# First attention rows behind the last down product, two query projections in the first group's slots

## The chip, the cores and the metric

One core of a Trainium2 chip. The metric is device microseconds for one execution of the whole kernel.

## The reference

x is 4 batches of 512 tokens of 512 values, ctx another such tensor. In four steps x gets:

```python
x = x + tanh(g_xattn[0]) * wkv_scan(layernorm(x), ctx)            # L0 attention
x = x + tanh(g_ffn[0])   * bitlinear_ffn(layernorm(x))            # w1, w2 (2048 wide), silu, w3
x = x + tanh(g_xattn[1]) * cross_attention(layernorm(x), ctx)     # L1, 16 heads of 32
x = x + tanh(g_ffn[1])   * ternary_linear(rmsnorm(layernorm(x)))

# cross_attention
q = qdq(x) @ qdq(wq).T + bq                   # qdq: round to int8 by the row's maximum, and back
k, v = split(cond @ wkv.T + bkv)
attn = softmax(einsum(q, k) * scale)
out = qdq(einsum(attn, v)) @ qdq(wp).T + bp
```

## The kernel before

Each engine has its program written out by hand in one function, and the engines are ordered by semaphores; every engine works strictly in its written order, so a wait holds all that is behind it on that engine.

The tokens are 16 row tiles (TOK) of 128. The first stage (to about 200 us) is the scan and the keys and values. The second is the two-layer network over the 16 tiles, tile by tile, with an `up` product in four pieces and a `down` product in four pieces. Under it, some tiles behind, run the query steps of the second attention for tile u: `q_stats` (mean and variance, VectorE), `q_rstd` (GpSimd), `q_norm` (ScalarE), `q_max` (row maximum, VectorE), `q_diag` (GpSimd), `q_round` (ScalarE), `q_ints` (VectorE), `q_turn` (TensorE transposes, and a product with ones that spreads the scale, bank 4), `q_operands` (ScalarE copies both out), `q_project` (16 matmuls of 128x128 on WQT, bank 7), `q_full` (VectorE, out of bank 7), `q_bias` (ScalarE, four pieces and a cast), `q_low` (GpSimd, the rest after rounding to 16 bits), `store_q` (SyncE, to DRAM). Tiles 13, 14 and 15 (TOK - 3 to TOK - 1) have these steps behind the network's end.

The third stage is the attention: 4 batches of 4 groups (b, g) of 4 heads, 16 groups, each with 16 slots (t, j), t a block of 128 keys and j a head. Ahead of a group, `rows` computes 16 products of queries and keys (banks 0, 1, 5 in turn) and VectorE's `maxima` takes the maximum of each (line 1682). `c_turn` (TensorE), `c_out` (ScalarE) and `c_low` (VectorE) make of them two rows c, which `send_c` (SyncE) puts beside the queries. In a slot, `scores` (line 1211) computes keys times queries with c and with the ones of `ones_under` (GpSimd) as further rows, ScalarE takes the exponential (line 957), `weigh` (line 1221) multiplies by the values, and GpSimd's `add_weights` (line 676) adds the exponentials of the four key blocks, head by head, 12 adds a group, into the buffers ACC. `sum_weights` (line 1233, slot 5 of the next group) sums them over the keys. The rows of the next group run in the slots (`coming`, 6 of them ahead). One rule ties the score of slot n to the exponential of slot n - 2, as there are two banks. The last stage (from about 830 us) is the output projection and the last linear layer.

The exponentials have eight buffers PR, the sums two sets ACC[0] and ACC[1], used by turns. Before, ACC[0] lies in low memory and ACC[1] in XQT, QF and QB, of which QF and QB are the buffers of `q_full` and `q_bias`. SyncE, once the last `up` product is done, loads keys, values and queries of the first batch's four groups, sends c of the first two groups, stores the queries of tiles 11 to 15, waits for the stores, and goes on with the loads of the next batch.

On TensorE, the order behind the last down product (tile 15) is `q_project(13)`, `q_turn(14)`, rows 0 to 2, `q_project(14)`, rows 3 and 4, `q_turn(15)`, rows 5 to 7, `q_project(15)`, rows 8 to 15, `c_turn(0, 0)`.

Of the kernel before, what the change touches and what calls it, by code (L numbers as in the profile page):

```python
# [60 lines left out]
def flamingo_kernel(nc, x, ctx_2048, g_xattn, g_ffn, w, u, w1, w2, w3, wq, bq, wkv, bkv, wp, bp, gamma, wl, out):  # L61
    stack = ExitStack()
    with stack:
# [61 lines left out]
        def part(count, dt, pat=None, **kw):  # L125
# [4 lines left out]
            if dt == F32:  # L130
# [57 lines left out]
        ACC = [[part(SEQ, F32) for _ in range(HG)],  # L188
               [a.bitcast(F32).rearrange("p n t -> p (n t)") for a in XQT] + [a.rearrange("p k t -> p (k t)") for a in (QF, QB)]]
# [152 lines left out]
        def _(sp):  # L342
# [152 lines left out]
            for u in range(TOK - DB - 1, TOK):  # L495
                store_q(u)
            sp.wait_ge(q_out, 32 * TOK)

            def feed(b, first, last):
                for g in range(DB):  # L500
                    at_b, at_g = (b, DB - 1) if g == 0 else (b + 1, g - 1)
                    if not (first and g == 0 or last and g > 0):
                        load_kv(at_b, at_g, False)
                        load_q(at_b, at_g)
                    if not (first and g == 0 or last and g == DB - 1):
                        send_c(*following(b, g))

# [12 lines left out]
        def _(pool):  # L520
# [125 lines left out]
            def ones_under(g):  # L646

                pool.wait_ge(b_ps, FC * TOK)
                pool.wait_ge(diag3, TOK)
                if g > 0:  # L650
                    pool.wait_ge(q_lo, TOK - DB + 1 + g)
                nc.gpsimd.memset(KS[96:98, HG * g:HG * g + HG, :], 1.0).then_inc(ks_ones, 1)
                pool.wait_ge(ks_ones, g + 1)
# [3 lines left out]
            q_low(TOK - 4)  # L657
            q_diag(TOK - 2)
            q_rstd(TOK - 1)
            q_diag(TOK - 1)  # L660
            ones_under(0)
            for u in (TOK - 3, TOK - 2, TOK - 1):
                q_low(u)
                ones_under(u - TOK + 4)

            def add_weights(b, first, last):
                for g in range(DB):
                    n, acc = b * DB + g, ACC[g % 2]
                    for t in range(1, TB - 1 if last and g == DB - 1 else TB):
                        for j in range(HG):  # L670
                            pool.wait_ge(exp_done, n * 16 + HG * t + j + 1)
                            if t == 1:
                                up_to(pool, sum_ps, n - 1)
                            else:
                                pool.wait_ge(acc_done, n * 12 + HG * (t - 2) + j + 1)
                            nc.gpsimd.tensor_tensor(acc[j], PR[j] if t == 1 else acc[j], PR[(HG * t + j) % 8],  # L676
                                                    ALU.add).then_inc(acc_done, 1)

# [21 lines left out]
        def _(act):  # L700
# [220 lines left out]
            q_operands(TOK - 1)  # L921
            q_bias(TOK - 2)
            q_bias(TOK - 1)
# [23 lines left out]
            def attend(b, first, last):  # L947
                for g in range(DB):
                    n = b * DB + g
                    opening, closing = first and g == 0, last and g == DB - 1  # L950
                    for t in range(TB):

                        up_to(act, pv_tile, n * TB + t - 1)
                        for j in range(HG):
                            up_to(act, acc_done, n * 12 + (j - 7, j - 3, j + 1, j + 1)[t])
                            act.wait_ge(st_ps, n * 16 + HG * t + j + 1)
                            nc.scalar.activation(PR[(HG * t + j) % 8], bank[2 + j % 2][:, :], ACT.Exp,  # L957
                                                 scale=SCALE).then_inc(exp_done, 1)
                            if (t, j) == (0, 3) and not opening:
                                ot_out(*preceding(b, g))  # L960
                            if (t, j) == (1, 3) and not opening:
                                sums_out(*preceding(b, g))
                            if (t, j) == (2, 1) and not closing:
                                c_out(*following(b, g))

# [51 lines left out]
        def _(pe):  # L1017
# [127 lines left out]
            def q_turn(u):  # L1145

                pe.wait_ge(li3, u + 1)
                up_to(pe, lt_out, u)
                for k in range(DB):
# [45 lines left out]
            def c_turn(b, g):  # L1195
                n = b * DB + g
                pe.wait_ge(row_max, n * 16 + 16)
                up_to(pe, den_ready, n - 2)
# [26 lines left out]
            def sum_weights(b, g, final=False):  # L1225

                n = b * DB + g
                pe.wait_ge(acc_done, n * 12 + (8 if final else 12))
                if not final:
# [37 lines left out]
            def attend(b, first, last):  # L1267
                for g in range(DB):
                    opening, closing = first and g == 0, last and g == DB - 1
                    ahead = coming(b, g)  # L1270
                    for slot in range(16):
# [6 lines left out]
                        if slot == 1 and not opening:  # L1278
                            weigh(*preceding(b, g), TB - 1)
                        if slot == 5 and not opening:  # L1280
# [18 lines left out]
            q_project(TOK - 3)  # L1299
            q_turn(TOK - 2)  # L1300
# [3 lines left out]
            q_project(TOK - 2)  # L1304
            first_rows(3, 5)
            q_turn(TOK - 1)
            first_rows(5, 8)
            q_project(TOK - 1)
            first_rows(8, 16)
            pe.wait_ge(down_read, TOK)  # L1310
            pe.wait_ge(h_done, FC * TOK)
            pe.wait_ge(qf_ready, TOK)
# [52 lines left out]
        def _(dve):  # L1365
# [341 lines left out]
            def attend(b, first, last):  # L1707
                for g in range(DB):
                    opening, closing = first and g == 0, last and g == DB - 1
                    ahead = coming(b, g)  # L1710
                    for slot in range(16):
# [4 lines left out]
                        if slot == 12:  # L1716
                            bias_row(b * DB + g)
                        if slot == 14 and not opening:
# [21 lines left out]
            q_full(TOK - 3)  # L1740
            link(ts(LSC, LSC, 1.0 / 127.0, None, ALU.mult))
            ts(LSC, LSC, TG[:, 3:4], None, ALU.mult).then_inc(area_free, 1)
            q_max(TOK - 1)
            first_maxima(0, 2)
            q_full(TOK - 2)
            q_ints(TOK - 1)
            first_maxima(2, 8)
            q_full(TOK - 1)
# [110 lines left out]
```

## Time and profile before

| | |
|---|---|
| median of 3 runs | 932.35 us (931.32 to 932.54) |
| the profiled execution | 932.0 us |
| its span | 930.3 us |
| mean granted clock of TensorE | 0.956 of full |
| busy TensorE, VectorE, ScalarE, GpSimd | 86%, 81%, 62%, 60% |

All times in rows are microseconds from the start of the span, of one profiled execution. In a row of a timeline the first number is the start, the second the time until the merged instructions (x4 is four) end, and in brackets stands the idle time of the engine ahead of them and what ended it. Matmul ends are modelled, and a row of one engine may overlap the next by the depth of its pipeline.

### The profile page before, as it was taken

The page shows a single profiled execution, that of the slowest core. Times are in us where ns is not written, and L with a number is a line of the kernel's source. Part 1 is how long each engine was busy: PE and PEld are TensorE (multiplying, and loading weights), DVE is VectorE, ACT ScalarE, POOL GpSimd, SP SyncE. Part 2 cuts the span into 40 slices and gives each one's busy share as a digit, 9 for nine tenths or more (in the row PEclk, how much of TensorE's full clock was granted, in tenths as well). Part 3 has the DMA queues.
Part 4 walks back from the last instruction along what each step waited for, and adds up shares of the span by engine and source line. Part 5 has one row for each costly group of instructions (what it writes and reads, how often), then busy time and mean ns, then how long its engine had stood idle before and what let it go on. Part 6 is the DMA issues. An engine that isn't in the chain of part 4 may idle for free.

```text
span 930.3 us, 14313 instructions
## 1 busy us (share of the span) xinstructions
PE 803.7 (86%) x4253; PEld 349.7 (38%) x4253; DVE 757.6 (81%) x1510; ACT 573.2 (62%) x974; POOL 553.6 (60%) x604
## 2 busy tenths in 40 slices
PE   3798997789999989999999987999999999855663
PEld 3454453334344444444444443232323232222221
DVE  4999998778899899899888768787888888634885
ACT  4878886543566565666666554666666666646762
POOL 7756753223334444444444344899999999955661
PEclk9999999799999999999999995999999999997886
DMA  9978875533353353354333455413131311000111
GB/s 306 248 203 221 220 184 162 135 88 69 61 120 58 79 114 77 72 80 80 80 69 71 77 119 109 102 47 92 47 92 47 91 47 47 2 1 0 46 68 68
DMA packets 186985, 90.70 MB, mean 97 GB/s; under 512 B 138640, under 2 KB 171552, under 8 KB 186912
## 3 DMA queue, kind: packets, MB, share of 16 engines
q1 hardware_dynamic: 186592, 89.82, 40.2%
q8 instruction: 33, 0.54, 0.3%
q14 instruction: 40, 0.33, 0.1%
q10 hardware_dynamic: 320, 0.01, 0.0%
HBM read 44.05 MB, written 16.78 MB: 65 GB/s over the span
## 4 chain that ended last, share of the span: by engine, by line
PE 34%; DVE 24%; issue 10%; ACT 7%; POOL 4%; DMA 0%; DVEq 0%; SPq 0%; ACTq 0%; POOLq 0%
PE bank L1129 11%; PE bank L1141 5%; PE bank L1221 4%; POOL B L676 4%; PE bank L1211 4%; PE bank L1192 4%; DVE bank L1556 3%; DVE gsm L1558 3%; DVE B L1567 3%; DVE B L1561 2%; DVE B L1682 2%; PE bank L1339 2%; ACT bank L830 2%; ACT A L957 2%; DVE gsm L1559 1%
## 5 line engine op out<-in xcount | busy, mean ns | idle before, releaser
L1129 PE MATMUL bank<-A,B 128*128 128x512 f16 x1024 | 233.1, 381 | 13.3 <-DVE B L1567 12.7
L607 POOL TENSOR_TENSOR B<-B 128x512 f16<-128x512 f32 x64 | 75.7, 1183 | 218.1 <-DVE B L1567 132.2
L1682 DVE TENSOR_REDUCE B<-bank 128x1 f32<-128x512 f32 x256 | 161.5, 682 | 42.5 <-PE bank L1192 42.2
L957 ACT ACTIVATE A<-bank 128x512 f32<-128x512 f32 x256 | 142.5, 602 | 81.9 <-PE bank L1211 79.8
L676 POOL TENSOR_TENSOR B<-B,A 128x512 f32<-128x512 f32 x124 | 160.6, 1330 | 0.0
L1129 PEld LDWEIGHTS bank<-A,B 128*128 128x128 f16 x1024 | 99.2, 98 | 139.3 <-DVE B L1567 15.7
L1141 PE MATMUL bank<-A,B 128*128 128x512 f16 x512 | 120.7, 379 | 0.0
L830 ACT ACTIVATE bank<-B 128x512 f32<-128x512 f32 x64 | 38.5, 602 | 130.5 <-DVE B L1561 130.5
L1211 PE MATMUL bank<-A 98*128 98x512 f16 x256 | 95.7, 386 | 9.8 <-ACT A L957 8.1
L1192 PE MATMUL bank<-A 96*128 96x512 f16 x256 | 98.6, 403 | 5.3 <-DVE B L1682 3.6
L676 POOL TENSOR_TENSOR B<-A 128x512 f32<-128x512 f32 x64 | 79.9, 1272 | 12.7 <-ACT A L957 12.3
L1221 PE MATMUL bank<-A,B 128*32 128x512 f32 x512 | 68.2, 604 | 2.4 <-ACT A L957 1.0
L1141 PEld LDWEIGHTS bank<-A,B 128*128 128x128 f16 x512 | 49.5, 98 | 54.3 <-DMA B<-B 0.4
L1104 PE MATMUL bank<-B 128*128 128x512 f16 x192 | 50.0, 416 | 20.0 <-DVE B L1448 19.9
L1556 DVE SCALAR_TENSOR_TENSOR bank<-bank,ffs,B 128x512 f32<-128x512 f32 x64 | 48.4, 755 | 12.9 <-PE bank L1129 11.6
L1567 DVE SCALAR_TENSOR_TENSOR B<-bank,gsm 128x512 f32<-128x512 f32 x64 | 44.2, 691 | 16.1 <-ACT bank L830 14.0
L825 ACT ACTIVATE B<-bank,ffs 128x512 f32<-128x512 f32 x64 | 43.2, 675 | 18.8 <-PE bank L1129 18.5
L559 POOL TENSOR_SCALAR B<-X,mv,rs 128x128 f32<-128x128 f32 x64 | 54.1, 858 | 0.4
L1192 PEld LDWEIGHTS bank<-A 96*128 96x128 f16 x256 | 25.1, 100 | 67.8 <-DVE B L1682 49.3
L593 POOL TENSOR_TENSOR B<-B 128x512 f16<-128x512 f32 x16 | 18.9, 1180 | 47.4 <-ACT B L804 40.3
L1211 PEld LDWEIGHTS bank<-A 98*128 98x128 f16 x256 | 24.9, 98 | 58.6 <-ACT A L957 38.3
L1558 DVE TENSOR_REDUCE gsm<-bank 128x8 f32<-128x512 f32 x64 | 44.3, 692 | 2.2
(215 smaller groups left out, 1463.7 us busy)
## 6 DMA issues: line engine op xcount, KB each, us to landing
B<-in_L_ffn_w_dram SPq DMA_DIRECT2D x48, 256.0 KB, 3.5
A<-k_parts SPq DMA_DIRECT2D x48, 128.0 KB, 2.6
A<-q_parts SPq DMA_DIRECT2D x48, 128.0 KB, 3.6
X<-in_x_dram SPq DMA_DIRECT2D x4, 1024.0 KB, 8.9
B<-in_ctx_dram SPq DMA_DIRECT2D x16, 256.0 KB, 5.2
k_parts<-B SPq DMA_DIRECT2D x16, 256.0 KB, 4.2
v_rows<-B SPq DMA_DIRECT2D x16, 256.0 KB, 2.7
q_parts<-B SPq DMA_DIRECT2D x32, 128.0 KB, 2.2
```

The lines of the kernel that those rows point to most:

```text
L607: nc.gpsimd.tensor_tensor(HLb[j][:, 1, :], Db[j % 2], HLb[j][:, 0, :], ALU.subtract).then_inc(lo_done, 1)
L676: nc.gpsimd.tensor_tensor(acc[j], PR[j] if t == 1 else acc[j], PR[(HG * t + j) % 8], ALU.add).then_inc(acc_done, 1)
L957: nc.scalar.activation(PR[(HG * t + j) % 8], bank[2 + j % 2][:, :], ACT.Exp, scale=SCALE).then_inc(exp_done, 1)
L1129: last = mm(bank[2 * n + q][:, :], XQT[a][:, m, :], wt[:, m % DB, j * 512:j * 512 + 512], start=(m == 0), stop=(m == 2 * DB - 1))
L1141: last = mm(bank[5 + q][:, :], HT[j][:, m, :], W3T[:, DB * j + m % DB, :], start=(j == 0 and m == 0), stop=(j == FC - 1 and m == 2 * DB - 1))
L1192: mm(bank[ROW_BANKS[r % 3]][:, :], QS[0:96, HG * g + j, t * P:t * P + P], KS[0:96, HG * g + j, :], start=True, stop=True).then_inc(row_ps, 1)
L1211: mm(bank[2 + j % 2][:, :], KS[0:98, HG * g + j, t * P:t * P + P], QS[0:98, HG * g + j, :], start=True, stop=True).then_inc(st_ps, 1)
L1221: last_ = mm(bank[6][DH * j:DH * j + DH, :], VB[:, t, (HG * g + j) * DH:(HG * g + j + 1) * DH], PR[(HG * t + j) % 8], start=(t == 0), stop ...
L1556: stt(H, H, C2, SAb[q], ALU.mult, ALU.mult).then_inc(h_done, 1)
L1558: link(reduce(gsm[:, 0, :], grouped(H), AX.X, ALU.max, apply_absolute_value=True))
L1567: stt(grouped(Db[q]), grouped(bank[q][:, :]), RND, spread(1), ALU.subtract, ALU.mult).then_inc(d_done, 1)
L1682: reduce(NMX[g % 2][:, t, j:j + 1], bank[ROW_BANKS[r % 3]][:, :], AX.X, ALU.max, negate=True).then_inc(row_max, 1)
```

## The change

TensorE now starts the first group's rows directly behind the last down product: rows 0 to 2, `q_project(13)`, rows 3 to 5, `q_turn(14)`, rows 6 to 15. `q_project(14)`, `q_turn(15)` and `q_project(15)` go to slots 2, 4 and 7 of the first group (`opening`). The steps of the other engines for these tiles follow into the slots, GpSimd's low part of tile 14 between its adds of t = 1 and t = 2 of the first group and that of tile 15 ahead of the second group's adds. As QF and QB are now in use during the first group, the buffers ACC move: ACC[1] takes WQT, which is free once `q_project(15)` is done. GpSimd's memsets of the ones come earlier, ahead of the low part of tile 13. SyncE stores tiles 14 and 15 behind the send of c for the third group.

```diff
-        ACC = [[part(SEQ, F32) for _ in range(HG)],
-               [... XQT] + [... (QF, QB)]]
+        low = [part(SEQ, F32) for _ in range(HG)]
+        wq_halves = WQT[:, :, :].rearrange("p k d -> p (k d)").bitcast(F32).rearrange("p (h s) -> p h s", h=2)
+        ACC = [low[0:2] + [a.bitcast(F32).rearrange("p n t -> p (n t)") for a in XQT],
+               low[2:4] + [wq_halves[:, h, :] for h in range(2)]]
...
@@ sync
-            for u in range(TOK - DB - 1, TOK):
+            for u in range(TOK - DB - 1, TOK - 2):
                 store_q(u)
-            sp.wait_ge(q_out, 32 * TOK)
...
                         send_c(*following(b, g))
+                    if first and g == 1:
+                        store_q(TOK - 2)
+                        store_q(TOK - 1)
+                        sp.wait_ge(q_out, 32 * TOK)
@@ gpsimd
             q_low(TOK - 4)
+            pool.wait_ge(q_lo, TOK - 3)
+            ones_under(0)
+            pool.wait_ge(ks_ones, 1)
             q_diag(TOK - 2)
             q_rstd(TOK - 1)
             q_diag(TOK - 1)
-            ones_under(0)
-            for u in (TOK - 3, TOK - 2, TOK - 1):
-                q_low(u)
-                ones_under(u - TOK + 4)
+            pool.wait_ge(diag3, TOK)
+            for g in range(1, DB):
+                ones_under(g)
+            pool.wait_ge(ks_ones, DB)
+            q_low(TOK - 3)
...
                     n, acc = b * DB + g, ACC[g % 2]
+                    if first and g == 1:
+                        q_low(TOK - 1)
+                        pool.wait_ge(qp_ps, TOK)
...
+                        if first and g == 0 and t == 1:
+                            q_low(TOK - 2)
@@ scalar
             q_bias(TOK - 3)
-            q_operands(TOK - 1)
-            q_bias(TOK - 2)
-            q_bias(TOK - 1)
...
+                            if (t, j) == (1, 1) and opening:
+                                q_operands(TOK - 1)
+                            if (t, j) == (1, 3) and opening:
+                                q_bias(TOK - 2)
+                            if (t, j) == (3, 1) and opening:
+                                q_bias(TOK - 1)
@@ tensor
+                if u == TOK - 1:
+                    pe.wait_ge(ct_ready, 1)
+                    pe.wait_ge(ct_low, 1)
...
                 pe.wait_ge(row_max, n * 16 + 16)
+                if n < 2:
+                    pe.wait_ge(lt_out, TOK - 1 + n)
...
                 pe.wait_ge(acc_done, n * 12 + (8 if final else 12))
+                if n == 0:
+                    pe.wait_ge(qf_ready, TOK)
...
+                        if slot == 2 and opening:
+                            q_project(TOK - 2)
+                        if slot == 4 and opening:
+                            q_turn(TOK - 1)
+                        if slot == 7 and opening:
+                            q_project(TOK - 1)
...
-            q_project(TOK - 3)
-            q_turn(TOK - 2)
             pe.wait_ge(d_done, FC * TOK)
             pe.wait_ge(down_read, TOK - 1)
             first_rows(0, 3)
-            q_project(TOK - 2)
-            first_rows(3, 5)
-            q_turn(TOK - 1)
-            first_rows(5, 8)
-            q_project(TOK - 1)
-            first_rows(8, 16)
+            q_project(TOK - 3)
+            first_rows(3, 6)
+            q_turn(TOK - 2)
+            first_rows(6, 16)
             pe.wait_ge(down_read, TOK)
             pe.wait_ge(h_done, FC * TOK)
-            pe.wait_ge(qf_ready, TOK)
             c_turn(0, 0)
@@ vector
+                        if slot == 3 and opening:
+                            q_ints(TOK - 1)
+                        if slot == 5 and opening:
+                            q_full(TOK - 2)
+                        if slot == 10 and opening:
+                            q_full(TOK - 1)
...
-            q_full(TOK - 3)
             link(ts(LSC, LSC, 1.0 / 127.0, None, ALU.mult))
             ts(LSC, LSC, TG[:, 3:4], None, ALU.mult).then_inc(area_free, 1)
+            first_maxima(0, 3)
             q_max(TOK - 1)
-            first_maxima(0, 2)
-            q_full(TOK - 2)
-            q_ints(TOK - 1)
-            first_maxima(2, 8)
-            q_full(TOK - 1)
+            first_maxima(3, 8)
+            q_full(TOK - 3)
             first_maxima(8, 16)
```

## Rows read from the trace of the kernel before

**Rows 1.** Waits, 584 to 830 us: who waited for whom; total, times, longest

```profile
POOL B L676 <- ACT A L957: 12.3, 14, 9.1
```

**Rows 2.** Timeline of GpSimd: the adds of groups 1 to 3

```profile
584.28 4.95 POOL L676 TENSOR_TENSOR B<-A 128x512 f32<-128x512 f32 x4 [9.12 <-ACT A L957]
589.20 10.74 POOL L676 TENSOR_TENSOR B<-B,A 128x512 f32<-128x512 f32 x8
599.89 4.99 POOL L676 TENSOR_TENSOR B<-A 128x512 f32<-128x512 f32 x4
...
615.12 2.50 POOL L676 TENSOR_TENSOR B<-A 128x512 f32<-128x512 f32 x2
```

**Rows 3.** Windows, one group long: length, busy time (count) of each engine, clock, DMA

```profile
599.90:615.45 15.55, 14.64 (x84) 4.61 (x88) 12.13 (x20) 10.09 (x19) 15.55 (x14) 1.00 0.40 111
```

**Rows 4.** The chain of waits, 568 to 580 us: start, length, what

```profile
568.75 4.79 DVE B L1682 x8
573.68 1.01 PE bank L1200 x4
...
575.85 0.59 DVE B L1690
...
579.10 0.61 PE bank L1211
```

**Rows 5.** Timeline of TensorE, 557 to 585 us

```profile
557.77 0.81 PE L1192 MATMUL bank<-A 96*128 96x512 f16 x3 [1.09 <-DMA A<-q_parts]
558.70 1.74 PE L1163 MATMUL bank<-B,WQT 128*128 128x128 f16 x16
...
563.84 0.61 PE L1150 MATMUL bank<-id,B 128*128 128x128 f16 x4 [2.54 <-DVE B L1595]
564.24 0.74 PE L1152 MATMUL bank<-B,ones 128*128 128x128 f32 x2
...
584.03 1.06 PE L1221 MATMUL bank<-A,B 128*32 128x512 f32 x8
```

**Rows 6.** Timeline of VectorE, 555 to 564 us

```profile
555.54 0.41 DVE L1595 TENSOR_SCALAR B<-B 128x512 f16<-128x512 f32 x1
...
558.04 0.69 DVE L1588 TENSOR_REDUCE B<-B 128x1 f32<-128x512 f32 x1 [1.18 <-ACT B L855]
...
562.16 0.69 DVE L1600 TENSOR_TENSOR B<-bank,B 128x512 f32<-128x512 f32 x1 [1.86 <-ACT B L876]
562.76 1.01 DVE L1595 TENSOR_SCALAR B<-B 128x512 f16<-128x512 f32 x1
```

**Rows 7.** Timeline of ScalarE, 559 to 573 us

```profile
559.15 0.72 ACT L859 ACTIVATE B<-B 128x512 f32<-128x512 f32 x1 [0.50 <-DVE B L1590]
...
565.01 0.58 ACT L865 COPY B<-bank 128x512 f16<-128x512 f16 x1 [2.96 <-PE bank L1152]
...
569.49 1.65 ACT L872 ACTIVATE B<-B,vec 128x128 f32<-128x128 f32 x4 [1.53 <-POOL B L625]
...
571.80 1.28 ACT L926 ACT_TABLE_LOAD   x1
```

**Rows 8.** Groups of ScalarE instructions, whole span: busy, mean ns, idle before

```profile
L993 ACT ACTIVATE bank<-X,mv 128x512 f32<-128x512 f32 x16 | 10.4, 682 | 5.5 <-DVE B L1790 5.5
```

**Rows 9.** Timeline of GpSimd, 562 to 564 us: the low part of tile 13

```profile
562.20 0.19 POOL L623 TENSOR_TENSOR held<-held 128x1 f32<-128x1 f32 x1 [0.69 <-ACT B L876]
562.34 1.15 POOL L625 TENSOR_TENSOR B<-B 128x512 f16<-128x512 f32 x1
```

**Rows 10.** Windows of TensorE: length, busy time, granted clock, DMA share, GB/s

```profile
553.50:557.70 4.20, 1.75 (x23) 1.00 1.06 230
...
563.80:568.90 5.10, 5.06 (x28) 0.50 1.15 218
568.90:572.60 3.70, 2.29 (x6) 0.96 0.18 36
...
579.10:582.80 3.70, 3.70 (x9) 0.50 0.00 0
```

More of the change, by code:

```diff
@@ L187, in flamingo_kernel @@
         OALL = part(TOK * D, F32, "p (t d) -> p t d", t=TOK)
-        ACC = [[part(SEQ, F32) for _ in range(HG)],
-               [a.bitcast(F32).rearrange("p n t -> p (n t)") for a in XQT] + [a.rearrange("p k t -> p (k t)") for a in (QF, QB)]]
+        low = [part(SEQ, F32) for _ in range(HG)]
+        wq_halves = WQT[:, :, :].rearrange("p k d -> p (k d)").bitcast(F32).rearrange("p (h s) -> p h s", h=2)
+        ACC = [low[0:2] + [a.bitcast(F32).rearrange("p n t -> p (n t)") for a in XQT],
+               low[2:4] + [wq_halves[:, h, :] for h in range(2)]]
         assert used[0] <= 20480
@@ L648, in ones_under @@
                 pool.wait_ge(b_ps, FC * TOK)
-                pool.wait_ge(diag3, TOK)
                 if g > 0:
-                    pool.wait_ge(q_lo, TOK - DB + 1 + g)
+                    pool.wait_ge(ks_ones, g)
                 nc.gpsimd.memset(KS[96:98, HG * g:HG * g + HG, :], 1.0).then_inc(ks_ones, 1)
-                pool.wait_ge(ks_ones, g + 1)
             q_diag(TOK - 3)
```

## The prediction

> **What bounds the kernel now.** I read the waits first, then the timeline of the attention stage, then the chain of waits, and last each engine's timeline between the last down product and the first attention group. The waits show that GpSimd's adds of the exponentials (line 676) stood idle for only 12.3 us in all, and that 9.1 us of this is one wait, before the very first add [rows 1]. The timeline shows the adds from 584.28 us on as one unbroken train: the second group's adds begin at 599.89, the third group's at 615.12, so a group is 12 adds in 15.2 to 15.6 us [rows 2]. TensorE is not far behind (14.64 us busy of 15.55) [rows 3], but the train of adds sets the end: whatever moves it moves the end one for one, as all later stages hang on its last group. So two things count: when the first add starts, and what is put among the adds afterwards.
>
> The first add is the end of a chain: the last row maxima, the turn of the maxima (573.68), the low part of c (575.85), the send of c by SyncE, the first score (579.10) [rows 4], five slots of scores and exponentials, and the add at 584.28 [rows 2]. Before that, VectorE is the long pole: 16 maxima at a pitch of 0.60 us (eight in 4.79) [rows 4], with the three query steps and their waits in between [rows 6].
>
> **The change, part by part.** *Up to the last row maximum.* The first rows can't start earlier: they wait for the load of the queries until 557.77 [rows 5], and nothing on the load queue ahead of that load moves. The projection of tile 13 and the turn of tile 14, which ran inside that wait, now come behind it. New order on TensorE: rows 0 to 2 at 557.77, projection 13 from 558.4 (1.74 us, as the one at 558.70) to 560.1, rows 3 to 5, turn 14 at 561.35 (1.14 us from 563.84 to the end of line 1152 at 564.98, to 562.5), rows 6 to 15 [rows 5]. VectorE: maxima 0 to 2 from 558.2 to 560.0, maximum of tile 15 with its two short steps 1.07 (as 558.04 to 559.1), maxima 3 to 5 from 561.1, one gap of 0.1 us for row 6 behind the turn, maxima 6 and 7 to 564.2, the copy of tile 13 0.60, maxima 8 to 15 in 4.9: done at 569.7. Before, they were done at 573.54 [rows 4]. The 3.8 us are the copies of tiles 14 and 15 (0.60 each), the rounding of tile 15 (1.01) and the wait of 1.86 us at 562.16, less odds [rows 6].
>
> The other engines keep up with this. ScalarE's operands of tile 14 now wait for the copy of tile 13 (564.8) and hold the rounding of tile 15 and bias 13 behind them: operands 0.85, rounding 0.7, bias and cast 2.3, table load 1.28 [rows 7] give 569.9, and the first thing wanted of it is the c copy at 570.8: 0.9 us of cover, and all beyond it would be late one for one. GpSimd has the memsets of the ones done at about 569 and the low part of tile 13 at about 570, with no add due for 11 us. SyncE puts the two stores of tiles 14 and 15 (four issues) behind the second group's sends; the third batch's loads that need them are far off, and the next batch's loads get earlier. The Exp table is loaded before two bias steps that use the Identity function; line 993 uses it after that load too, and no load follows the one at 571.80, so I cost this at nothing (the other bound is 1.28 a load) [rows 7, 8].
>
> The steps from the last maximum to the first score took 5.56 us (573.54 to 579.10) [rows 4] and are unchanged: first score at 575.3, 3.8 earlier.
>
> *From the first score to the first add.* This took 5.18 us, of which the first 3.7 at TensorE's lower clock [rows 2, 4, 10]. Projection 14 now stands behind the third score. I take the rise of the clock where it was, counted from the first score, as TensorE is again busy without a gap from there: of the 16 matmuls 11 run at 0.107 us and 5 at about half, 1.5 us in all. Slots 3 and 4 at the full clock: fourth score 579.7, fifth 580.15, their exponentials one behind the other (0.6 each), first add at 581.25. So of 3.8 us 3.0 are left. The price of the projection lies between 0 (under the exponentials) and 1.74.
>
> *Within the first group.* Here the adds wait for things of the change, and each wait is on the path. (1) Turn 15 behind the fifth score needs VectorE's rounding of tile 15, which comes behind the maxima of slot 3: 580.9, done 581.3 at 0.41. Turn to 582.0, row, sixth score at 582.2, its exponential 582.6 to 583.2. The first add ends at 582.5: 0.7 idle. (2) ScalarE's operands 15 wait for the copy of tile 14, which on VectorE is behind the maximum of slot 5: 583.6, operands to 584.45; behind them the next exponential to 585.05 where the second add ended at 584.45: 0.6 idle. (3) Bias 14 (2.3) from 585.65 to 587.9; the fourth add ends at 587.55 and the low part of tile 14 waits 0.4. (4) That low part takes 0.15 and 1.15 on GpSimd [rows 9]: 1.3. Sum: 1.7 idle and 1.3 work; bounds are 0 (the exponentials keep ahead) and 1.7, doubled if each engine queues behind the other. The eight remaining adds take 10.3 if like a later group (15.23 less four of 1.23), 10.69 as before (589.20 to 599.89) [rows 2]; I take 10.3, as the trace has one add of 2.1 us here that no later group has. The group's adds end at 599.6, 0.3 earlier than 599.89. Bias 15 falls where exponentials are ahead of the adds; its cover is the eight adds.
>
> *Second group.* The low part of tile 15 stands ahead of its adds: 1.3 again, bare, as the train has no slack: adds from 600.95 where they began at 599.89. The projection, turn and copies themselves cost nothing more, since TensorE waited in this group for the adds anyway. From here nothing is changed (other buffers for the sums are the same size in the same memory).
>
> Sum: -3.0 + 1.7 + 1.3 - 0.4 + 1.3 = +0.9, by the times above +1.06; say **+1.0 us**. The profiled execution took 932.0 us (span 930.3 and 1.7 around it), so 933.0; the median of the runs, 932.35, is 0.35 above it: I predict **933.3**. Two low parts and three pauses moved from where GpSimd was idle into the one train that isn't idle eat what the earlier start gives.
>
> *A rule weighed.* The rounding of tile 15 took 1.01 us while GpSimd's low part (562.34) ran and 0.41 mostly [rows 6, 9]. The Trainium skill (GPSIMD Engine Reference, Key points) says that GpSimd shares its SBUF interfaces with VectorE, with contention when VectorE is in a two-port mode or reads two SBUF inputs. By that rule a rounding that starts after the first add waits it out; without it the sum stands at +1.0.
>
> **The rivals.** *The rounding of tile 15 meets the first add.* In my times it starts 0.35 us before the add. Started after it, it takes 0.6 more (as 1.01 against 0.41) up to a whole add, 1.25, and the turn, the sixth score and all that follows move with it: +1.6 to +2.3, about 934.3. For it: 0.35 us is little. Against: both hang on the same two rows, so their order is firm.
>
> *The clock stays low: the slower side.* Place: slots 4 to 7 of the first group. TensorE waits about 1 us for the rounding behind slot 4. If the clock has not risen by then (580.4), the turn costs 0.5 more, the eight weighing matmuls of slot 5 (1.06 at the full clock [rows 5]) 1.0 more, two rows and scores 0.4 each: the seventh exponential is 2 to 2.5 later, and with it the low part of tile 14: +3.5, 935.8. It decides if the rise comes more than 1.4 us later than I set it. For: the clock was low for most of the 25 us ahead; against: both spells of unbroken work shown ended at the full clock [rows 10]. The Trainium skill (TensorE: Matmul & The Clock Gate, Part 1) says that the throttled state is the default and that activity releases it; the trace agrees, and the pause of 4.2 us that TensorE now has ahead of the first rows would by that rule put them at the lower clock too.
>
> *The clock is up at the first score: the faster side.* Projection 13, rows and turn 14 are one unbroken spell now (557.8 to 562.5), and single rows follow. If the clock is still up at 569.7, the turn is 0.4 shorter and its row 0.1, and slots 0 to 4 take 4.25 instead of 5.95 us: first add at 579.05, -1.1 in all, 931.2. Against: such single rows (2.29 us busy of 3.7) ended in a fall of the clock at 572.6 [rows 10].
>
> *The adds don't pause.* If exponentials and query steps interleave better than my in-order reading, the 1.7 us go: -0.7, 931.6; with the clock up as well -2.8, 929.5.
>
> *The change does not do what it says.* If bias 13 and the table load run over the 0.9 us of cover, the c copy is late and part of 3.8 us is lost: 0.5 to 1 us more, within the range.
>
> **How the numbers follow.** Forecast 0.38, rounding meets the add 0.16, clock low 0.15, clock up 0.14 (alone 0.08, with no pauses 0.06), no pauses 0.12, late table load 0.05. Range 929.7 to 936.3, which cuts only the ends of the clock cases. A measurement of this kernel can tell about 0.2%, 1.9 us, from no change. Slower by more: all of clock low (0.15), half of rounding (0.08), a tail of the forecast (0.05): 0.28. Faster by more: clock up with no pauses (0.06), and parts of clock up alone and of no pauses (0.1), where my 3.8 us could be larger: 0.16. Same: 0.56.
>
> **What would show it.** The first score near 575.3, the first add near 581.3; in the first group's adds three pauses and the low part between the fourth and the fifth; the second group's adds behind the low part of tile 15, about 1 us later than 599.89; from there the train as before. Wrong if the first add is before 579.5 or after 583, if there are no pauses, or if the group pitch behind 616 is no longer 15.5.

## The result, and the profile after

The changed kernel takes 939.07 us (median of 7 runs, 936.27 to 941.99), the kernel before 932.35: a ratio of 1.0076, with a 95% interval of 1.0058 to 1.0093. It is slower by 6.7 us; 933.3 was forecast, and the range ended at 936.3.

Where a profiled execution stands when the first row begins differs by up to 8 us between executions of any of these kernels (552 to 560 us), which comes from the stages ahead of it. So I compare stretches from the start of the first row (557.77 before [rows 5], 552.77 after):

| from the first row to | before | forecast | after |
|---|---|---|---|
| first score | 21.33 | 17.5 | 17.28 |
| first add of GpSimd | 26.51 | 23.5 | 23.58 |
| second group's first add | 42.12 | 43.2 | 43.33 |
| third group's first add | 57.35 | 58.4 | **65.85** |
| end of the last group's adds | 269.6 | 270.7 | **278.1** |

Up to the second group's first add the forecast holds within 0.25 us; then 7.4 us go in one group, and stay. The stretch is 8.5 us longer and the median 6.7; with starts that differ by up to 8 us, the rest can't be placed. GpSimd's timeline of the kernel after, to set beside [rows 2] (line 630 is the low part, 686 the add):

```profile
576.35 1.27 POOL L686 TENSOR_TENSOR B<-A 128x512 f32<-128x512 f32 x1 [11.61 <-ACT A L966]
578.26 1.27 POOL L686 TENSOR_TENSOR B<-A 128x512 f32<-128x512 f32 x1 [0.64 <-ACT A L966]
580.10 2.50 POOL L686 TENSOR_TENSOR B<-A 128x512 f32<-128x512 f32 x2 [0.57 <-ACT A L966]
582.75 0.20 POOL L628 TENSOR_TENSOR held<-held 128x1 f32<-128x1 f32 x1 [0.15 <-ACT B L888]
582.90 1.15 POOL L630 TENSOR_TENSOR B<-B 128x512 f16<-128x512 f32 x1
584.01 10.86 POOL L686 TENSOR_TENSOR B<-B,A 128x512 f32<-128x512 f32 x8
594.84 0.18 POOL L628 TENSOR_TENSOR held<-held 128x1 f32<-128x1 f32 x1
594.99 1.15 POOL L630 TENSOR_TENSOR B<-B 128x512 f16<-128x512 f32 x1
596.10 2.49 POOL L686 TENSOR_TENSOR B<-A 128x512 f32<-128x512 f32 x2
...
608.37 2.47 POOL L686 TENSOR_TENSOR WQT<-WQT,A 128x512 f32<-128x512 f32 x2
618.62 2.50 POOL L686 TENSOR_TENSOR B<-A 128x512 f32<-128x512 f32 x2 [7.79 <-ACT A L966]
```

The three pauses of the first group are there, and both low parts. The pause that nobody had foreseen is the 7.79 us ahead of 618.62. What made it is on VectorE (line 1705 is the row maximum, 1760 the bias add `bias_row`, 1618 the rounding of tile 15); the second fence is TensorE from the same view:

```profile
575.97 0.41 DVE L1618 TENSOR_SCALAR B<-B 128x512 f16<-128x512 f32 x1
...
585.70 0.67 DVE L1760 TENSOR_TENSOR X<-X,bp_all 128x512 f32<-128x512 f32 x1
...
601.74 9.65 DVE L1760 TENSOR_TENSOR X<-X,bp_all 128x512 f32<-128x512 f32 x1
611.31 1.28 DVE L1705 TENSOR_REDUCE B<-bank 128x1 f32<-128x512 f32 x2
```

```profile
612.05 0.61 PE L1210 MATMUL bank<-A 96*128 96x512 f16 x1 [6.68 <-DVE B L1705]
```

The bias add of row 1 of X, in slot 12 of the second group, took 9.65 us; the median of the 16 is 1.07, as it was before. It ended (611.39) only when GpSimd's adds of the group had ended (610.84, the end of the row at 608.37), 0.55 us behind the last of them. While it stood, no row maximum ran behind it, so TensorE's rows waited 6.68 us for their banks, the scores behind them waited, the exponentials ran out, and with them the adds of the third group. It is a ring: VectorE gets in when GpSimd's train breaks, and the train breaks when the work that VectorE holds up runs out.

### The profile page after: what moved, and what is told of

It is laid out like the page before. It is cut to its first block, busy times and chain, and to the rows that moved or that the text cites. A ratio compares the mean times of both kernels' runs of the same rounds, so it can differ in the third digit from the quotient of the medians.

```text
span 934.6 us, 14314 instructions
## 1 busy us (share of the span) xinstructions
PE 801.9 (86%) x4253; PEld 349.0 (37%) x4253; DVE 765.5 (82%) x1510; ACT 572.8 (61%) x974; POOL 553.9 (59%) x604
## 4 chain that ended last, share of the span: by engine, by line
PE 35%; DVE 25%; issue 10%; ACT 6%; POOL 3%; DMA 1%; SPq 1%; DVEq 0%; ACTq 0%; POOLq 0%
PE bank L1144 10%; PE bank L1156 5%; PE bank L1241 4%; PE bank L1210 4%; PE bank L1231 4%; DVE B L1705 3%; DVE bank L1579 3%; DVE gsm L1581 3%; DVE B L1590 3%; POOL B L686 2%; PE bank L1362 2%; DVE B L1584 2%; ACT bank L842 2%; ACT A L966 2%; PE bank L1255 1%
## 5 line engine op out<-in xcount | busy, mean ns | idle before, releaser
L1144 PEld LDWEIGHTS bank<-A,B 128*128 128x128 f16 x1024 | 99.1, 98 | 138.5 <-DVE B L1590 15.8
L686 POOL TENSOR_TENSOR B<-B,A 128x512 f32<-128x512 f32 x94 | 120.9, 1315 | 0.0
L686 POOL TENSOR_TENSOR B<-A 128x512 f32<-128x512 f32 x48 | 60.0, 1270 | 22.6 <-ACT A L966 22.1
L1119 PE MATMUL bank<-B 128*128 128x512 f16 x192 | 45.9, 390 | 20.5 <-DVE B L1471 20.5
L837 ACT ACTIVATE B<-bank,ffs 128x512 f32<-128x512 f32 x64 | 43.3, 676 | 15.8 <-PE bank L1144 15.5
```

The costliest lines, as they stand in the source:

```text
L1144: last = mm(bank[2 * n + q][:, :], XQT[a][:, m, :], wt[:, m % DB, j * 512:j * 512 + 512], start=(m == 0), stop=(m == 2 * DB - 1))
```

## The experiments

The stretch is from the first row to the end of the last group's adds, of one profiled execution; the ratio is to the kernel before as measured beside each variant, with its interval; the hold is the longest bias add. e2, e4, e5, f1, g1, h1 to h4 and i1 are variants of the kernel before, the others of the changed one.

| kernel | stretch | hold | median us | ratio |
|---|---|---|---|---|
| e1_row1_late | 271.0 | 1.09 | 931.89 | 1.0005 (0.9986 to 1.0023) |
| e2_before_wqt | 270.7 | 1.07 | 931.06 | 0.9993 (0.9975 to 1.0011) |
| e3_memset | 279.3 | 9.61 | 940.70 | 1.0084 (1.0058 to 1.0111) |
| e4_shift | 270.9 | 1.22 | 933.08 | 1.0001 (0.9974 to 1.0027) |
| f1_before_pad | 270.3 | 1.07 | 931.60 | 1.0004 (0.9981 to 1.0027) |
| f2_slot13 | 279.3 | 9.05 | 942.60 | 1.0110 (1.0058 to 1.0163) |
| f3_break | 271.2 | 1.12 | 933.97 | 1.0027 (1.0006 to 1.0047) |
| g1_pad_f16 | 279.1 | 9.51 | 938.27 | 1.0079 (1.0049 to 1.0109) |
| g2_drain | 272.4 | 1.21 | 932.65 | 1.0021 (0.9999 to 1.0043) |
| g3_low_later | 279.5 | 9.29 | 940.74 | 1.0103 (1.0076 to 1.0131) |
| h1_pad_f32 | 278.8 | 9.38 | 945.15 | 1.0140 (1.0089 to 1.0190) |
| h2_pad_f16_only | 277.8 | 9.38 | 941.98 | 1.0106 (1.0056 to 1.0156) |
| i2_slot13_late | 278.0 | 8.45 | 942.67 | 1.0095 (1.0061 to 1.0129) |
| h4_sum7_only | 276.8 | 9.57 | 937.78 | 1.0062 (1.0042 to 1.0081) |
| i1_sum7_drain | 268.7 | 1.55 | 929.99 | 0.9976 (0.9957 to 0.9996) |
| e5_before_poolbias | 268.1 | none | 932.55 | 1.0005 (0.9990 to 1.0019) |
| e6_after_poolbias | 269.5 | none | 933.15 | 1.0022 (1.0004 to 1.0039) |
| h3_before_sum7 | 267.0 | none | 929.01 | 0.9968 (0.9947 to 0.9989) |

The three pads g1, h1 and h2 were run twice each, f2 and g3 four times, so their medians are rough; the argument rests on the holds and the stretches. The medians go with them all the same: 937.8 to 945.2 us where an add was held, the changed kernel among them, and 929.0 to 934.0 where none was.

**Is it this one instruction?** The changed kernel with the bias of row 1 added behind the attention:

```diff
-                        if slot == 12:
+                        if slot == 12 and not (first and g == 1):
                             bias_row(b * DB + g)
...
+            bias_row(1)
             def scales(n, m):
```

> The changed kernel, but VectorE adds the bias to row 1 of X behind the attention and no longer in slot 12 of the second group, where this one instruction took 9.65 us in the trace of the changed kernel. Nothing is left out. Theory PORT (VectorE's add of two SBUF operands waits for GpSimd's train of adds to break): the 7.3 us that the train of adds lost there come back, 932.35 + 1 = about 933.4, and the third group's adds begin about 16.2 us less 0.4 behind the second group's, not 22.5. Rival BUFFER (the sums in WQT are what slows the second group): the stall stays, about 939.

The 7 us are back and no other bias add took over the hold. The third group's adds begin 14.7 us behind the second's, where 15.8 was expected: twelve adds back to back. The time lies 1.5 us under what was expected, and the changed kernel without the hold can't be told from the kernel before.

**Is it the place of the sums?** The kernel before with the four lines on `ACC` of the change alone:

> The kernel before with only the buffers of the sums moved as in the changed kernel (ACC[1] partly in WQT). Nothing is left out. PORT: nothing changes, 932.3 within 1 us, and every bias add of VectorE takes 0.67 to 1.1 us. BUFFER: the stall of 9 us appears in a group of odd number, 936 to 940.

Nothing changed: BUFFER falls.

**Is it the moment within an add?** In the changed kernel the bias add was issued 0.72 us behind the start of an add, in the kernel before 0.75 to 0.77 us in groups 2 to 14. One memset ahead of it moves it by a little:

```diff
+                            if first and g == 1:
+                                nc.vector.memset(held[:, 2:3], 0.0)
                             bias_row(b * DB + g)
```

> The changed kernel with one memset of 1 element (59 ns) on VectorE ahead of the bias add of row 1. Nothing is left out. PORT with a narrow window: the bias add was issued 0.72 us behind the start of a GpSimd add when it was held, and 0.74 to 0.77 us when it was let in at the add's end; 0.06 us later it falls on the good side, and the time is about 933.4. If it is the stage and not the offset that holds it (rival BUFFER, or the low part ahead of the train), it stays about 939.

Held all the same, issued at 0.75 us. And from the other side, a tiny GpSimd add ahead of t = 2 in every group of the kernel before:

```diff
+                        if t == 2:
+                            nc.gpsimd.tensor_tensor(held[:, 0:1], held[:, 1:2], held[:, 1:2], ALU.add)
```

> The kernel before with one tiny GpSimd add (0.14 to 0.19 us) ahead of the t = 2 adds of every group. The output is the reference's. Alone it costs 16 x 0.15 = 2.4 us if the adds set the pitch: about 935. It shifts GpSimd against VectorE's bias add by 0.15 us in every group: if the offset within an add decides, bias adds are held in several groups, 7 us each: above 945. If not, 933 to 935.

The moment moved to 0.60 us and nothing was held: the bias adds took 1.22 us. The moment within the add doesn't decide.

**Is it which add runs?** The hold began in the first add of t = 2, the short waits in the second. Slot 13, and then slot 13 with one reduction more ahead of it (the reduction is in the second only):

```diff
-                        if slot == 12:
+                        if slot == (13 if first and g == 1 else 12):
+                            if first and g == 1:
+                                reduce(OM[:, 15:16], bp_all[:, :], AX.X, ALU.max)
                             bias_row(b * DB + g)
```

> The changed kernel with the bias add of row 1 one slot later, in slot 13, behind that slot's row maximum. Nothing is left out. If what decides is which add runs when VectorE asks (the hold began in the first add of t = 2, the short waits in the second), it now falls one or two adds later and takes 1.07 us: about 933.4. If the stretch decides, it is held again: 936 to 939, for as long as the train lasts from there.

> The changed kernel with the bias add of row 1 in slot 13 and one VectorE reduction of 0.6 us more ahead of it (its result is overwritten), so that the request falls 0.6 to 0.8 us behind the start of the second add of t = 2, where the kernel before has its requests. Nothing is left out. If the add that runs when VectorE asks decides: 1.07 us, stretch 271 to 272, 934. If GpSimd's unbroken train decides: held for 7 to 9 us, 278 to 279, 940.

In the second, the request came 0.73 us into the second add of t = 2, just where the kernel before has its requests, and was held for 8.45 us. So it isn't the add either. VectorE's timeline of this kernel:

```profile
603.83 0.66 DVE L1741 TENSOR_REDUCE B<-bp_all 128x1 f32<-128x512 f32 x1
604.42 8.45 DVE L1762 TENSOR_TENSOR X<-X,bp_all 128x512 f32<-128x512 f32 x1
```

**Does a pause of GpSimd let it in?** The changed kernel with a wait for the bias ahead of the third add of t = 2:

```diff
+                            if first and (g, t, j) == (1, 2, 2):
+                                pool.wait_ge(x_biased, 2)
```

> The changed kernel with one wait more: GpSimd stops ahead of the third add of t = 2 of the second group until row 1 has its bias. Nothing is left out. PORT (VectorE gets in only where GpSimd's train breaks): the bias add ends 1.3 to 1.9 us after its start at the latest, the train loses 0.6 to 1.2 us instead of 7.3, and the time is 934 to 934.6. If the bias add took 9.65 us by itself and not by GpSimd's work, the train would lose all of that: about 941.

```profile
606.99 1.12 DVE L1762 TENSOR_TENSOR X<-X,bp_all 128x512 f32<-128x512 f32 x1
```

```profile
608.19 2.49 POOL L688 TENSOR_TENSOR WQT<-WQT,A 128x512 f32<-128x512 f32 x2 [0.63 <-DVE X L1762]
```

Same slot, same data, same engines busy: 1.12 us in place of 9.65, and 0.63 us of the train. This shows that it was GpSimd's unbroken train that held VectorE.

**What makes the train unbroken?** First a pad of one add in the kernel before, with a wait for its end:

```diff
+                    if first and g == 1:
+                        for _ in range(1):
+                            step.link(nc.gpsimd.tensor_tensor(acc[3], bp_all[:, :], bp_all[:, :], ALU.add))
```

> The kernel before with one GpSimd add of 128x512 (1.25 us, its result is overwritten) ahead of the second group's adds, where the changed kernel has the low part of tile 15. The output is the reference's. The steps of the change are all absent but this delay of GpSimd against the other engines by one add. Theory LATE TRAIN (a GpSimd that runs one add behind the other engines keeps VectorE's bias add out until its train breaks): the second group's bias add takes 9 to 10 us and the time is 932.5 + 1.3 + 7, about 940. Rival (another piece of the change is needed for it): 933.8, bias add 1.07 us.

Not held (0.93 us), and the theory LATE TRAIN, as I had put it, fell. The pad however brought its own wait. So a stand-in that doesn't wait for its own end (the wait for `qp_ps`, the end of the last projection, had long been met: that projection ran at 564.10 to 566.01):

```diff
+                    if first and g == 1:
+                        pool.wait_ge(qp_ps, TOK)
+                        nc.gpsimd.tensor_tensor(held[:, 0:1], held[:, 1:2], held[:, 1:2], ALU.add)
+                        nc.gpsimd.tensor_tensor(WQT[:, 0, :], bp_all[:, :], bp_all[:, :], ALU.add)
```

> The kernel before with a stand-in for the low part of tile 15 ahead of the second group's adds: one tiny GpSimd add and one of 128x512 with a 16-bit result into the free WQT, and no wait for their end, so that GpSimd's train is not broken there. The output is the reference's. If the unbroken low part is what makes VectorE's bias add wait for the whole train, the second group's bias add takes 9 to 10 us here too and the stretch from the first row to the end of the last add is 269.6 + 1.3 + 7 = 278. If it needs another piece of the change: bias add 0.7 to 1.1 us, 270 to 271.

GpSimd (672 is the stand-in) and VectorE in this kernel, which has nothing else of the change:

```profile
598.14 1.04 POOL L672 TENSOR_TENSOR WQT<-bp_all 128x512 f16<-128x512 f32 x1
599.13 4.95 POOL L680 TENSOR_TENSOR B<-A 128x512 f32<-128x512 f32 x4
604.03 9.84 POOL L680 TENSOR_TENSOR B<-B,A 128x512 f32<-128x512 f32 x8
622.40 2.50 POOL L680 TENSOR_TENSOR B<-A 128x512 f32<-128x512 f32 x2 [8.54 <-ACT A L961]
```

```profile
604.90 9.51 DVE L1735 TENSOR_TENSOR X<-X,bp_all 128x512 f32<-128x512 f32 x1
```

The hold, made in the kernel before by two GpSimd operations, one of them tiny. The reverse is the changed kernel with one wait behind the low part of tile 15:

```diff
                         q_low(TOK - 1)
+                        pool.wait_ge(q_lo, TOK)
```

> The changed kernel with one wait more: GpSimd waits for the end of the low part of tile 15 before it starts the second group's adds (about 0.1 us of pause). Nothing is left out. If the hold needs a train that is unbroken from the low part on: bias add 0.7 to 1.1 us, 933.5. If it depends on how late GpSimd is against the others: held again, 939.

```profile
595.50 1.16 POOL L630 TENSOR_TENSOR B<-B 128x512 f16<-128x512 f32 x1
596.73 2.50 POOL L687 TENSOR_TENSOR B<-A 128x512 f32<-128x512 f32 x2
```

```profile
602.26 1.21 DVE L1761 TENSOR_TENSOR X<-X,bp_all 128x512 f32<-128x512 f32 x1
```

The next add starts 1.23 us behind the low part, not 1.11 as in the changed kernel, and this 0.12 us, 5.5 us ahead of the request, is enough (1.21 us, a little over the 1.1 expected). GpSimd is as late against the other engines here as in the changed kernel (its third add starts 1.44 us behind its exponential, 1.34 there), so its lateness doesn't decide. Next the low part moved out of the second group's way:

```diff
-                        q_low(TOK - 1)
...
+                        if first and g == 1 and t == 3:
+                            q_low(TOK - 1)
```

> The changed kernel with the low part of tile 15 behind the second group's adds of t = 2 and not ahead of its first. Nothing is left out. If the low part ahead of the bias add (as a break of the order, or by making GpSimd late) is the cause: bias add 0.7 to 1.1 us, from the first row to the last add's end 270.7 to 271, about 933. If the stretch alone is: 278, about 939.

The edit put it behind the last adds of the group, so ahead of the third group's first add, and not behind t = 2 as the expectation has it. The second group's bias add was let in (1.07 us), as expected; the third group's, the first behind the moved low part, was held, which was not. The hold moves with the low part:

```profile
613.23 1.16 POOL L630 TENSOR_TENSOR B<-B 128x512 f16<-128x512 f32 x1
614.35 4.95 POOL L685 TENSOR_TENSOR B<-A 128x512 f32<-128x512 f32 x4
```

```profile
620.33 9.29 DVE L1761 TENSOR_TENSOR X<-X,bp_all 128x512 f32<-128x512 f32 x1
```

Two more pads, without the tiny add, to see whether it or the 16-bit result matters (each with the same two lines ahead of it as in g1):

```diff
...
+                        nc.gpsimd.tensor_tensor(WQT[:, 0:2, :].rearrange("p k d -> p (k d)").bitcast(F32), bp_all[:, :], bp_all[:, :], ALU.add)
```

> The kernel before with one GpSimd add of 128x512 with a 32-bit result into the free WQT ahead of the second group's adds, with no wait for its end and no tiny add. The output is the reference's. If any further add without a wait in the train does it: the second group's bias add takes 9 to 10 us, stretch from the first row to the last add's end 278 to 279. If a 16-bit result or the tiny add is needed: 0.7 to 1.2 us and 270 to 271.

```diff
...
+                        nc.gpsimd.tensor_tensor(WQT[:, 0, :], bp_all[:, :], bp_all[:, :], ALU.add)
```

> The same with a 16-bit result, still without the tiny add. The output is the reference's. If the 16-bit result does it: 9 to 10 us and 278 to 279. If the pair of tiny and large add does it: 0.7 to 1.2 us and 270 to 271.

Both held, 9.38 us: one add more in the train did it each time, where no wait came with it.

**Does it need a pad at all?** In each later group of the kernel before GpSimd pauses ahead of the third add, 0.14 to 0.30 us, until an exponential comes, because TensorE does the sums of the preceding group in slot 5. With the sums in slot 7 (and their copy on ScalarE at t = 2, j = 1) that pause goes or moves:

```diff
-                        if slot == 5 and not opening:
+                        if slot == 7 and not opening:
                             sum_weights(*preceding(b, g))
```

> The kernel before with the sums in slot 7 alone, bias adds where they were. Nothing is left out. GpSimd has 15.24 us of work a group here, so the pitch can fall from 15.54 to 15.25 at most: 15 x 0.3 = 4 us off, 928 to 929, if the ring sets it; 932 if not. The bias add may meet a longer unbroken train: if the hold of 9 us appears in some group, 7 us each on top.

```profile
600.04 4.96 POOL L676 TENSOR_TENSOR B<-A 128x512 f32<-128x512 f32 x4
604.96 9.82 POOL L676 TENSOR_TENSOR B<-B,A 128x512 f32<-128x512 f32 x8
622.87 4.97 POOL L676 TENSOR_TENSOR B<-A 128x512 f32<-128x512 f32 x4 [8.09 <-ACT A L957]
```

No operation was added to GpSimd here, only waits taken away, and the second group is held (9.57 us). The bias adds of the groups behind it, each with a pause of 0.2 to 0.5 us at its start, are let in. With one wait of GpSimd for its own last add at each group's start:

```diff
+                    up_to(pool, acc_done, n * 12)
                     for t in range(1, TB - 1 if last and g == DB - 1 else TB):
```

> The kernel before with the sums in slot 7 and, at the start of each group's adds, a wait of GpSimd for the end of its own last add. Nothing is left out. The variant without this wait had the second group's bias add held for 9.57 us and its stretch at 276.8. If a pause of about 0.1 us within the group is enough to let VectorE in: no bias add above 1.3 us, stretch 269 to 270, 931 to 932. If not: 277, 938.

```profile
597.71 4.96 POOL L677 TENSOR_TENSOR B<-A 128x512 f32<-128x512 f32 x4
...
613.02 4.95 POOL L677 TENSOR_TENSOR B<-A 128x512 f32<-128x512 f32 x4
...
628.34 4.96 POOL L677 TENSOR_TENSOR B<-A 128x512 f32<-128x512 f32 x4
```

No hold (the longest bias add took 1.55 us), and 929.99 us: faster than the kernel before by a little, 0.24%. The groups shown are 15.3 us long, most of the later ones 15.5.

**What the bias adds cost, and what sets the pitch.** All of them on GpSimd under the network's tiles, in the kernel before and in the changed one, and the former with the sums in slot 7:

```diff
+            def bias_row(u):
+                pool.wait_ge(lx_done, u + 1)
+                row_ = X[:, bass.ds(u, 1), :].rearrange("p a d -> p (a d)")
+                nc.gpsimd.tensor_tensor(row_, row_, bp_all[:, :], ALU.add).then_inc(x_biased, 1)
...
+                        if j == 0 and there(i - 3):
+                            bias_row(i - 3)
```

> The kernel before with the bias adds taken off VectorE's slots in the attention and given to GpSimd under the network's tiles, three tiles behind, where GpSimd is half idle (1.25 us each), the last three behind its memsets. Nothing is left out. PORT: each bias add in the attention made one add of GpSimd longer (one of 1.7 us among 1.23), 0.45 us in each of 16 groups; these come back as far as TensorE (14.7 to 14.9 us busy of 15.5) lets them: 0.3 to 0.45 us a group, 925 to 928. If TensorE's loop sets the pitch, 931 to 932. If GpSimd's adds hold up the network's low parts, above 933.

> The changed kernel with all bias adds given to GpSimd under the network's tiles, as in the variant of the kernel before. Nothing is left out. There that took 7.7 us off GpSimd's adds and 1.5 us off the stretch from the first row to the last add's end, as the pitch of the groups stayed at 15.5. PORT: nothing of two SBUF operands is left on VectorE in the attention, so no hold: 932.35 + 1.1 - 1.5, within 1 us of 932. Rival (the hold is not of this instruction): 938 to 939.

> The kernel before with the bias adds under the network's tiles (as the earlier variant), and the sums of the preceding group in slot 7 in place of slot 5 on TensorE, their copy on ScalarE one step of t later. Nothing is left out. If the pitch of 15.5 us is set by the ring of sums behind the last add, two slots of scores, and the exponentials that the next adds wait for (0.7 us of GpSimd idle a group), it falls to what GpSimd or TensorE need, 14.8 to 15.0: 15 x 0.55 = 8 us off, 923 to 926. If it is set by something else: 931 to 933.

The costliest groups of the first of these, and one window of it about a group long:

```profile
L685 POOL TENSOR_TENSOR B<-B,A 128x512 f32<-128x512 f32 x124 | 152.9, 1273 | 0.0
```

```profile
631.50:647.00 15.50, 14.75 (x86) 4.64 (x84) 11.39 (x20) 10.25 (x20) 14.73 (x13) 1.00 0.26 69
```

These adds were 160.6 us in the kernel before. That is 7.7 us less over 16 groups, GpSimd is busy for 14.73 us of the window, and a group is still 15.5 us long. The changed kernel without any bias add in the attention has no hold either (its time is 0.15 us above what I allowed). In the kernel before, the expected 925 to 928 was missed, and with it the reading that GpSimd's train alone sets the pitch. With the sums in slot 7 the gain is 3.4 us by the medians, not the 6 to 9 expected. The profiled executions show less of it: the stretch is 1.0 us shorter than without that step (267.0 and 268.1), 0.4 us of it in the second group, and the third to the fourteenth are 15.4 to 15.8 us long in both. So the place of the sums is a small part of the pitch at most; what holds it at 15.5 I haven't settled.

## Why the prediction was wrong

*Up to the last row maximum and the first score*: right. 17.28 us against 17.5; the order worked out engine by engine was the order of the trace, with ScalarE's operands of tile 14 waiting for the copy of tile 13 and the table load ending ahead of the c copy.

*From the first score to the first add*: right. TensorE stood at its lower clock there and projection 14 ran in it:

```profile
570.05:573.80 3.75, 3.75 (x18) 2.10 (x19) 2.94 (x5) 1.79 (x3) 0.00 (x0) 0.50 0.00 0
573.80:576.35 2.55, 1.79 (x12) 0.94 (x10) 1.59 (x4) 1.08 (x2) 0.00 (x0) 0.89 0.00 0
```

The rise came behind 3.75 us of unbroken work, as before [rows 10], and both clock rivals fell: not up at the first score (0.50), not low in slots 4 to 7 (1.00 from 576.35 to 579.00). For the first rows the prediction named a lower clock behind the longer pause: the granted clock was 1.00 in the 4.2 us ahead of them and 0.75 in their first 2.2 us, and both figures were the same before.

*Within the first group*: right in kind. Pauses of 0.64, 0.57 and 0.15 against 0.7, 0.6 and 0.4. The eight adds took 10.83 (584.01 to 594.84) where I had taken 10.3 as "the trace has one add of 2.1 us here that no later group has". That add of 2.1 us was the bias add of this group going in ahead of GpSimd, and it came again.

*The rounding of tile 15*: began at 575.97, 0.38 us ahead of the first add (0.35 forecast), and took 0.41; that rival fell.

*Second group*: this step failed. I priced the low part of tile 15 at its own 1.3 us, "bare, as the train has no slack", and wrote "from here nothing is changed". The 1.3 us are right (43.33 against 43.2). Wrong was that the train had no slack, and that taking it costs nothing: "one unbroken train" passed over thirteen further waits of 3.2 us in all (12.3 less 9.1 [rows 1]), and each bias add let in among the adds came behind such a wait (below). Before, the third add of the second group began as soon as its exponential was there (0.60 us from 601.70, so 602.30):

```profile
601.70 0.60 ACT L957 ACTIVATE A<-bank 128x512 f32<-128x512 f32 x1 [2.85 <-PE bank L1211]
602.37 1.28 POOL L676 TENSOR_TENSOR B<-A 128x512 f32<-128x512 f32 x1
```

With GpSimd 1.3 us later, no add waits for anything (the third starts 1.34 us behind the end of its exponential), and VectorE's bias add, which I had never costed, stood for 9.65 us: +7.3 us (618.62 less the 611.33 that 596.10 and the 15.23 us of [rows 2] give).

*The rule weighed*: right rule, wrong instruction. I weighed the shared access between GpSimd and VectorE for the one instruction that the change puts next to the adds, and not for those that stood there already, one in each group, though the row with 1.0 us against 0.4 [rows 6] showed that such waits happen. The Trainium skill (SBUF — State Buffer, section "SBUF: two separate sides") says that the shared pair of ports is an exclusive lock, and that whichever of the two starts first has it for the whole instruction. A price worked out by that page is an estimate: the bias add waits for one add at most, 1.2 us. The trace doesn't agree, as the hold here outlasted seven further adds. The measurement decides.

*What bounds the kernel*: right for this change, as what delayed the train moved the end one for one (1.2 us of low part and 7.3 of hold, and the stretch 8.5 longer). Too strong as a statement on the pitch, as the variant with 7.7 us less of adds showed.

*Open*: how the train keeps VectorE out. What counts as a break can be read from the 17 kernels with bias adds on VectorE, 272 of them in all. An add that waited for its exponential starts 0.08 us behind the exponential's end, whether the pause before it can be seen or not: 617.92 in the kernel before, with an idle time of 0.30 us, and 602.37, with none. By this sign, 261 of the 263 bias adds that weren't held were asked for behind an add of the same group that had waited, for an exponential or for another engine's or its own last result. The other two are f3_break, where the wait came right behind the request, and the bias add that e1_row1_late put behind the attention, which met the very last add. In the nine held groups (the changed kernel, four variants of it, the three pads, and the sums in slot 7) no add up to the request had waited: each started at least 0.99 us behind its exponential. How many adds a train must have, and what in GpSimd's queue keeps the access, no run here tells.

## What to carry to other kernels

On an engine with hardly any slack, an operation put into the train costs its own length and the pauses that it swallows: look up who depends on these pauses, above all VectorE instructions that read two operands in SBUF beside a busy GpSimd. In a profile the sign is one instruction of a group with a maximum far above its median. A wait of GpSimd for its own last result cost 0.12 us and kept a hold of 9 us away, once in the changed kernel (g2_drain) and once a group in the kernel before with the sums in slot 7 (i1_sum7_drain); or take such VectorE operations out of the stage (e6_after_poolbias).

## What the hardware showed that I had not expected

- A VectorE add of two SBUF operands of 128x512 (0.67 us at its shortest) took 8.45 to 9.65 us beside an unbroken train of GpSimd adds, in nine kernels, and ended each time 0.55 us behind the last add of the train.
- With a pause of 0.12 us in the train, 5.5 us ahead of the request, it took 1.21 us.
- When it goes in beside a running add (first group, asked for 0.35 to 0.47 us behind the add's start), the next add starts 2.11 to 2.23 us behind the running one, in place of 1.23. When it waits for the running add's end, it is the next add that takes 1.67 to 1.73 us to the start of the one behind it.
